# Transformer block on one core: batch 0's keys get a bank of their own, its parts are made by two engines, and the fillers read a cleared tile

## The chip, the cores and the metric

One core of one Trainium2 chip runs the whole program. The metric is the device time of one execution in microseconds (us). Most of the program is steady: one batch of sixteen takes some 12.2 us. The change touches only the head, the first 15 us or so, in which the weights arrive and batch 0 is brought to its first attention scores.

## The reference, cut to what matters

```python
mod = (silu(L0_c) @ L0_wmod).reshape(16, 6, 1, -1)
sa, ca, ga, sb, cb, gb = (mod[:, i] for i in range(6))
h = layernorm(x) * (1 + ca) + sa                  # x: 16 batches x 256 tokens x 128
qkv = (h @ Wqkv + bqkv).reshape(b, t, 3, H, HD).transpose(2, 0, 3, 1, 4)   # 16 heads of 8
q, k, v = qkv
dist2 = sum(k*k)[..., :, None] + sum(q*q)[..., None, :] - 2.0 * einsum(k, q)
x = x + ga * (einsum(exp(-dist2 * r_sigma), v) @ Wproj + bproj)
h = layernorm(x) * (1 + cb) + sb
x = x + gb * (sum over the two best of eight experts of h @ w_e.T + b_e)
```

## The kernel before, in words

Every engine has its own instruction list, written out by hand, and the engines meet at semaphores. Each list runs strictly in the order in which it is written, so a waiting instruction holds back everything behind it. `step(k)` is called on every engine for k = -2 (batch 0's first layer norm), k = -1 (batch 0's queries, keys, values and score operands) and then once per batch, k being the batch whose attention is done.

The exponent is computed by one matmul per head. For that the kernel builds `st`, which stacks for each head the rounded queries and keys ("high", fp32r), what the rounding left ("low"), and the halved negative squared norms of both, which a matmul with the constant matrix `nw` sums from `sq`. High and low parts lie in `hl` (rows 0 and 1 queries, 2 and 3 keys), the norms in `norm_hi` and `norm_parts`. For batch 0 the steps are, on the critical way:

- PE fills its waits with matmuls whose result nobody reads (`warm_up`, line 913), transposes the conditioning vector (L920), multiplies it with the modulation weights (L925), transposes the normalised batch (L1034).
- DVE turns the modulation into `shift_col` and `scale_col` (L626, L627). ACT makes `h1` from them and the transposed batch (L553).
- PE computes queries and keys into one PSUM bank, `qkv_ps` (L1000: four strips for the queries, then four for the keys), and the values into `ffn_ps` (L1009).
- DVE adds the bias columns `bqk_col` (L714, `qkf`), ACT rounds (L475), DVE squares (L639), subtracts (L641), and PE sums the squares (L1022), DVE makes `norm_hi` and `norm_parts` (L726, L731).
- Five DMAs from the queues of SP and ACT (L310, L312, L317, L484, L488) carry the parts into `st`. PE's first scores (L961) wait for all five.

The constants in between are DVE's too: `bias_columns` (L643 to L659) multiplies the identity with the bias loaded by L292 (`bq_pick`, L646), sums it to `bqk_col` (L652) and makes `nw`, `lo_col`, `be_col` and `ident_r` from the identity alone. DVE also clears the value tile `vpad` of batch 0 (L902), and POOL that of batch 1.

## Time and profile before

| | us |
|---|---|
| median of three runs (lowest, highest) | 225.71 (224.12, 226.25) |
| the profiled execution, its own time | 226.44 |
| its span, first to last instruction | 224.6 |
| outside the span | 1.84 |
| PE busy | 210.0 (93% of the span) |
| DVE, ACT, POOL busy | 174.8, 163.5, 137.3 |

The profile lists each instruction or a merged run of them with its start, its length and what released the engine. One matmul of fp32 data shows as two records. "Idle before" is what the engine waited for. The chain of waits follows the last instruction back to its releaser, step by step, and so names what set the time.

### The profile page before, as it was taken

The numbers are of one execution on the slowest core, as the hardware profiler recorded it, in microseconds if no ns is written. First come the engines' busy times: TensorE is split into PE (matmuls) and PEld (weight loads), VectorE is DVE, ScalarE is ACT, GpSimd is POOL, SyncE is SP. The second block draws the span as 40 slices with busy tenths as digits, with TensorE's granted clock in tenths as the row PEclk, the third lists the DMA queues.
The fourth block names the chain that finished last, engine by engine and source line by source line (L and its number), as shares of the span: only waits on it lengthen the run. The fifth ranks groups of instructions, "written<-read, shape, count | busy, mean of one in ns | idle before, by whom it ended". The sixth has DMA issues, their size and how long they took to land.

```text
span 224.6 us, 8205 instructions
## 1 busy us (share of the span) xinstructions
PE 210.0 (93%) x3240; PEld 150.1 (67%) x3240; DVE 174.8 (78%) x610; ACT 163.5 (73%) x234; POOL 137.3 (61%) x204
## 2 busy tenths in 40 slices
PE   7986888899999999999999999999999999999993
PEld 7653444577776767777677767676776776766792
DVE  4775441868888897988897888979888988787884
ACT  5228688877786868798777878686978777777362
POOL 5455547474866757575849577675757594435183
PEclk9997899999999999999999999999999999999999
DMA  5562424332423333434333243324242323300001
GB/s 149 149 206 99 146 87 121 117 109 84 120 85 115 95 136 86 146 90 146 92 125 93 78 128 103 118 77 149 88 148 69 140 62 107 99 23 26 3 23 48
DMA packets 22472, 22.94 MB, mean 102 GB/s; under 512 B 2330, under 2 KB 20258, under 8 KB 22434
## 3 DMA queue, kind: packets, MB, share of 16 engines
q1 hardware_dynamic: 21962, 21.79, 30.6%
q10 hardware_dynamic: 472, 0.62, 0.8%
q8 instruction: 26, 0.43, 0.8%
q14 instruction: 12, 0.10, 0.1%
HBM read 6.65 MB, written 2.12 MB: 39 GB/s over the span
## 4 chain that ended last, share of the span: by engine, by line
PE 69%; DVE 18%; issue 4%; DMA 3%; ACT 2%; SPq 1%; POOL 1%; POOLq 0%; ACTq 0%
PE att_ps L981 25%; PE qkv_ps L1000 8%; PE scores L961 7%; DVE acc L708 5%; DVE eq L787 4%; PE qkv_ps L1119 3%; PE qkv_ps L1009 3%; DMA st<-norm_parts 3%; PE scores L913 2%; DVE topi L784 2%; PE mid_ps L1083 2%; DVE x_all L746 2%; ACT probs L495 2%; PE qkv_ps L1121 2%; PE qkv_ps L1120 2%
## 5 line engine op out<-in xcount | busy, mean ns | idle before, releaser
L495 ACT ACTIVATE probs<-scores 128x1024 f32<-128x1024 f32 x128 | 124.3, 1022 | 12.8 <-PE scores L961 7.7
L981 PE MATMUL att_ps<-probs,vpad 128*32 128x256 f32 x1024 | 69.1, 386 | 0.0
L981 PEld LDWEIGHTS att_ps<-probs,vpad 128*32 128x32 f32 x1024 | 31.4, 110 | 16.9 <-issue 1.0
L961 PE MATMUL scores<-st 32*128 32x256 f32 x512 | 37.7, 331 | 4.6 <-ACT probs L495 2.7
L368 POOL TENSOR_TENSOR ve<-stats,eps 128x2 f32<-128x2 f32 x32 | 6.2, 193 | 43.4 <-DVE stats L688 43.4
L961 PEld LDWEIGHTS scores<-st 32*128 32x128 f32 x512 | 23.3, 184 | 13.8 <-ACT probs L495 4.7
L708 DVE SCALAR_TENSOR_TENSOR acc<-ffn_ps,mask,acc 128x128 f32<-128x128 f32 x114 | 32.0, 342 | 0.2
L411 POOL TENSOR_TENSOR sq<-qkf 128x512 f32<-128x512 f32 x15 | 15.6, 1040 | 24.6 <-DVE qkf L714 24.6
L375 POOL TENSOR_SCALAR xn<-x_all,stats,rstd 128x128 f32<-128x128 f32 x30 | 25.5, 853 | 1.6
L708 DVE SCALAR_TENSOR_TENSOR acc<-qkv_ps,mask,acc 128x128 f32<-128x128 f32 x64 | 18.0, 344 | 9.5 <-PE qkv_ps L1121 9.5
L370 POOL TENSOR_TENSOR rstd<-ve,expo 128x2 f32<-128x2 f32 x32 | 22.6, 707 | 2.5
L714 DVE TENSOR_TENSOR qkf<-qkv_ps,bqk_col 128x512 f32<-128x512 f32 x16 | 11.1, 692 | 12.5 <-PE qkv_ps L1000 12.5
L413 POOL TENSOR_TENSOR hl<-qkf,hl 128x512 fp32r<-128x512 f32 x15 | 19.4, 1290 | 0.8 <-DVE hl L720 0.8
L1000 PE MATMUL qkv_ps<-h,wqk_sb 128*32 128x256 f32 x256 | 18.0, 401 | 0.0
L502 ACT COPY acc<-mid_ps 128x256 f32<-128x256 f32 x15 | 5.6, 372 | 17.0 <-PE mid_ps L1083 17.0
L1119 PE MATMUL ffn_ps<-we_hi,h_hi 128*128 128x256 f32 x56 | 17.0, 304 | 0.0
L1120 PE MATMUL ffn_ps<-we_hi,h_lo 128*128 128x256 f32 x56 | 15.6, 278 | 0.0
L1121 PE MATMUL ffn_ps<-we_lo,h_hi 128*128 128x256 f32 x56 | 15.5, 278 | 0.0
L756 DVE TENSOR_SCALAR x2n<-x_all,stats,rstd 128x128 f32<-128x128 f32 x32 | 9.7, 344 | 7.5 <-POOL rstd L370 7.5
L708 DVE SCALAR_TENSOR_TENSOR acc<-att_ps,mask,acc 128x128 f32<-128x128 f32 x52 | 14.6, 342 | 0.2 <-DVE acc L708 0.2
L382 POOL TENSOR_TENSOR gated<-acc,rb_all 128x256 f32<-128x256 f32 x14 | 10.3, 734 | 5.2 <-DVE acc L708 4.5
L688 DVE BATCH_NORM_STATS2 stats<-x_all 128x6 f32<-128x256 f32 x32 | 12.4, 420 | 0.1
(170 smaller groups left out, 428.5 us busy)
## 6 DMA issues: line engine op xcount, KB each, us to landing
st<-hl SPq DMA_DIRECT2D x47, 256.0 KB
rb_all<-rb_rows SPq DMA_DIRECT2D x16, 192.0 KB, 3.2
out_dram<-x_all SPq DMA_DIRECT2D x16, 128.0 KB, 1.9
x_all<-in_L_attn_x_dram SPq DMA_DIRECT2D x13, 128.0 KB, 3.2
st<-norm_parts SPq DMA_DIRECT2D x60, 16.0 KB
we_sb<-in_L_ffn_w_experts_dram SPq DMA_DIRECT2D x1, 512.0 KB, 5.8
w_mod_sb<-in_L_wmod_dram SPq DMA_DIRECT2D x1, 256.0 KB, 5.1
st<-hl ACTq DMA_DIRECT2D x1, 256.0 KB
```

What stands on the lines that cost most here:

```text
L370: nc.gpsimd.tensor_tensor(rstd[:, n, :], ve[:, n, :], expo[:, :], ALU.pow).then_inc(rstd_ok, 1)
L375: i = nc.gpsimd.tensor_scalar(xn[:, par, t * C:(t + 1) * C], x_all[:, b, t * C:(t + 1) * C], stats[:, 0, par, 3 * t + 1:3 * t + 2], rstd[: ...
L411: nc.gpsimd.tensor_tensor(sq[:, :, :], qkf[:, :, :], qkf[:, :, :], ALU.mult).then_inc(sq_ok, 1)
L413: nc.gpsimd.tensor_tensor(hl[:, 1:4:2, :], qkf[:, :, :], hl_f[:, 0:4:2, :], ALU.subtract).then_inc(lo_ok, 1)
L495: nc.scalar.activation(probs[:, g, 2 * half:2 * half + 2, :], scores[:, 2 * half:2 * half + 2, :], ACT.Exp, scale=two_sigma).then_inc((exp ...
L708: v.scalar_tensor_tensor(acc[:, q, t, :], y, m, acc[:, q, t, :], ALU.mult, ALU.add).then_inc(acc_step, 1)
L961: i = pe.matmul(scores[:, r, t * T:(t + 1) * T], st[rows, par, g, t * P:(t + 1) * P], st[rows, par, g, T:2 * T], start=True, stop=True)
L981: i = pe.matmul(att_ps[r * ROWS:(r + 1) * ROWS, 0:T], heads[:, g * ROWS:(g + 1) * ROWS], probs[:, g, r, t * T:(t + 1) * T], start=(g == 0 ...
L1000: i = pe.matmul(qkv_ps[m, a * T:(a + 1) * T], wqk_sb[:, a, m], h1[:, :], start=True, stop=True)
L1119: pe.matmul(dst, hi, we_hi[:, es], start=True, stop=False)
L1120: pe.matmul(dst, lo, we_hi[:, es], start=False, stop=False)
L1121: i = pe.matmul(dst, hi, we_lo[:, es], start=False, stop=True)
```

## The change

1. For batch 0 the queries' bank stays `qkv_ps`, the keys go to `att_ps`, and the norm sums to bank 0 of `scores`. PE signals after the four query strips (`q0_ps`) and again after the four key strips (`qk_ps`).
2. DVE makes the queries' parts from PSUM in four instructions of 256 columns. ACT makes the keys' square and high part from PSUM, and also `norm_hi`. DVE makes the keys' low part. The bias enters each instruction as a column.
3. The seven fillers at the start (four before) and all later ones read `blank`, which DVE clears as its first act. They no longer wait for the identity. Two fillers ahead of `norms(0)` go.
4. `nw`, `lo_col`, `be_col`, `ident_r` are made right after the identity. `bq_pick` moves ahead of the modulation's columns, `bqk_col` stays behind batch 1's statistics.
5. The clearing of `vpad` for batch 0 goes from DVE to POOL. ACT doubles and loads sigma before the key parts, not after its DMAs. `turn_x(1)` waits for `lo_ok` in place of `v_ok` and `norm_ok`, and the expert transposes wait for `lo_ok` too.

```diff
+        def k_bank(b):
+            return att_ps[:, 0:T] if b == 0 else qkv_ps[:, T:2 * T]
+        def n_bank(b):
+            return scores[:, 0, :] if b == 0 else qkv_ps
         def norm_tile(b):
...
+                if b == 0:
+                    sp.wait_ge(hi0_ok, 1)
...
+                    if k == -2:
+                        nc.gpsimd.memset(vpad[:, 0, :, :, :].rearrange("p t h w -> p (t h w)"), 0.0).then_inc(vpad_ok, 1)
...
-            def high_parts():
-                act.wait_ge(qkf_ok, 1)
-                nc.scalar.copy(hl[:, 0:4:2, :], qkf[:, :, :]).then_inc(hi_ok, 1)
+            def first_keys():
+                act.wait_ge(qk_ps, 1)
+                act.wait_ge(bqk_ok, 1)
+                nc.scalar.activation(sq[:, 1, :], k_bank(0), ACT.Square, bias=bqk_col[:, 1:2]).then_inc(sq_ok, 1)
+                nc.scalar.activation(hl[:, 2, :], k_bank(0), ACT.Identity, bias=bqk_col[:, 1:2]).then_inc(hi_ok, 1)
...
             def norm_high(b):
...
-                nc.scalar.copy(norm_hi[norm_tile(b)], qkv_ps[norm_tile(b)]).then_inc(nh_ok, 1)
+                nc.scalar.copy(norm_hi[norm_tile(b)], n_bank(b)[norm_tile(b)]).then_inc(nh_ok, 1)
...
             def first_low_rows():
-                act.wait_ge(lo_ok, 1)
+                act.wait_ge(hi_ok, 1)
+                act.wait_ge(lo0_ok, 1)
...
-                    high_parts()
...
+                    act.wait_ge(sig_ok, 1)
+                    nc.scalar.reg_load(two_sigma, sig[0:1, 1:2].bitcast(U32))
+                    first_keys()
+                    norm_high(0)
...
-                    act.wait_ge(sig_ok, 1)
-                    nc.scalar.reg_load(two_sigma, sig[0:1, 1:2].bitcast(U32))
...
             def first_parts():
...
+                dve.wait_ge(q0_ps, 1)
+                dve.wait_ge(bqk_ok, 1)
+                v.tensor_scalar(qkf[:, 0, :], qkv_ps[:, 0:T], bqk_col[:, 0:1], None, ALU.add).then_inc(qkf_ok, 1)
...
-                v.tensor_tensor(sq[:, :, :], qkf[:, :, :], qkf[:, :, :], ALU.mult).then_inc(sq_ok, 1)
+                v.scalar_tensor_tensor(sq[:, 0, :], qkv_ps[:, 0:T], bqk_col[:, 0:1], qkf[:, 0, :], ALU.add, ALU.mult).then_inc(sq0_ok, 1)
+                v.tensor_scalar(hl[:, 0, :], qkv_ps[:, 0:T], bqk_col[:, 0:1], None, ALU.add).then_inc(hi0_ok, 1)
+                dve.wait_ge(hi0_ok, 1)
+                v.scalar_tensor_tensor(hl[:, 1, :], qkv_ps[:, 0:T], bqk_col[:, 0:1], hl_f[:, 0, :], ALU.add, ALU.subtract).then_inc(lo0_ok, 1)
...
-                v.tensor_tensor(hl[:, 1:4:2, :], qkf[:, :, :], hl_f[:, 0:4:2, :], ALU.subtract).then_inc(lo_ok, 1)
-            def bias_columns():
+                v.scalar_tensor_tensor(hl[:, 3, :], k_bank(0), bqk_col[:, 1:2], hl_f[:, 2, :], ALU.add, ALU.subtract).then_inc(lo_ok, 1)
+            def bias_picks():
...
-                v.tensor_reduce(nw_pick[:, :, :], ident[:, :].rearrange("p (r d g) -> p r g d", r=R, d=HD), AX.X, ALU.add).then_inc(nw_pick_ok, 1)
+            def bias_columns():
...
+            def norm_columns():
+                v.tensor_reduce(nw_pick[:, :, :], ident[:, :].rearrange("p (r d g) -> p r g d", r=R, d=HD), AX.X, ALU.add).then_inc(nw_pick_ok, 1)
+                v.tensor_reduce(lo_col[:, :], ident[:, :].rearrange("p (m i g) -> p i m g", i=2, g=G)[:, 1, :, :], AX.XY, ALU.add, negate=True).then_inc(nw_ok, 1)
+                v.tensor_reduce(be_col[:, :], ident[:, NE:2 * NE], AX.X, ALU.add, negate=True).then_inc(nw_ok, 1)
...
-                v.tensor_reduce(lo_col[:, :], ident[:, :].rearrange("p (m i g) -> p i m g", i=2, g=G)[:, 1, :, :], AX.XY, ALU.add, negate=True).then_inc(nw_ok, 1)
-                v.tensor_reduce(be_col[:, :], ident[:, NE:2 * NE], AX.X, ALU.add, negate=True).then_inc(nw_ok, 1)
...
              def queries_keys(b):
-                if b == 0:
-                    dve.wait_ge(bqk_ok, 1)
...
             def norm_rows(b):
-                dve.wait_ge(n_ps, b + 1)
-                if b == 0:
-                    v.tensor_copy(norm_hi[norm_tile(b)], qkv_ps[norm_tile(b)]).then_inc(nh_ok, 1)
...
-                v.scalar_tensor_tensor(norm_parts[tile], norm_hi[tile].bitcast(F32), lo_col[tile[0], :], qkv_ps[tile],
+                v.scalar_tensor_tensor(norm_parts[tile], norm_hi[tile].bitcast(F32), lo_col[tile[0], :], n_bank(b)[tile],
...
             def values(b):
...
-                if b == 1:
-                    dve.wait_ge(vpad1_ok, 1)
+                if b < 2:
+                    dve.wait_ge((vpad_ok, vpad1_ok)[b], 1)
...
+                    bias_picks()
...
-                if k == -1:
-                    queries_keys(k + 1)
-                if k == -1:
...
+            v.memset(blank[:, :], 0.0).then_inc(blank_ok, 1)
...
-            v.memset(vpad[:, 0, :, :, :].rearrange("p t h w -> p (t h w)"), 0.0).then_inc(vpad_ok, 1)
+            norm_columns()
...
             def warm_up(n, w=P):
...
-                    pe.matmul(scores[:, R - 1, 0:w], ident[:, :], ident[:, 0:w], start=True, stop=True)
+                    pe.matmul(scores[:, R - 1, 0:w], blank[:, :], blank[:, 0:w], start=True, stop=True)
...
             def modulation():
+                pe.wait_ge(blank_ok, 1)
+                warm_up(6)
+                warm_up(1, P // 2)
...
-                warm_up(3)
-                warm_up(1, P // 2)
...
+                pe.wait_ge(lo_ok, 1)
...
+                    dst = (qkv_ps[:, 0:T], k_bank(b))[a]
...
-                        i = pe.matmul(qkv_ps[m, a * T:(a + 1) * T], wqk_sb[:, a, m], h1[:, :], start=True, stop=True)
+                        i = pe.matmul(dst[m, :], wqk_sb[:, a, m], h1[:, :], start=True, stop=True)
+                    if b == 0 and a == 0:
+                        i.then_inc(q0_ps, 1)
...
             def values(b):
...
             def norms(b):
...
+                    pe.wait_ge(sq0_ok, 1)
...
-                    i = pe.matmul(qkv_ps[j * ROWS:(j + 1) * ROWS, tokens], nw[:, :, :, :].rearrange("p r i g -> p (r i g)"),
+                    i = pe.matmul(n_bank(b)[j * ROWS:(j + 1) * ROWS, tokens], nw[:, :, :, :].rearrange("p r i g -> p (r i g)"),
...
             def turn_x(b):
...
-                    pe.wait_ge(v_ok, b)
-                    pe.wait_ge(norm_ok, b)
+                    pe.wait_ge(lo_ok, b)
...
             def start():
...
-                warm_up(2)
```

DVE's list around batch 0's modulation and parts, before. Names are the tiles of the section above, `ld_bq` is the load of the bias, `mod_ps` the modulation's matmul.

```order
L626 COPY shift_col<-mid_ps 128x16 [waits mod_ps]
L627 TENSOR_SCALAR scale_col<-mid_ps 128x16
L688 BN_STATS stats<-x_all 128x6 [waits ld_x0]
L646 TENSOR_TENSOR bq_pick<-ident,bq_all 128x128 [waits ld_bq]
L646 TENSOR_TENSOR bq_pick<-ident,bq_all 128x128
L650 TENSOR_REDUCE nw_pick<-ident 128x16
L652 TENSOR_REDUCE bqk_col<-bq_pick 128x2 [waits bq_pick_ok]
L655 TENSOR_SCALAR nw<-nw_pick 128x4x4 [waits nw_pick_ok]
L655 TENSOR_SCALAR nw<-nw_pick 128x4x4
...
L714 TENSOR_TENSOR qkf<-qkv_ps,bqk_col 128x512 [waits bqk_ok,qk_ps]
L639 TENSOR_TENSOR sq<-qkf 128x512 [waits qkf_ok]
L641 TENSOR_TENSOR hl<-qkf,hl 128x2x256 [waits hi_ok]
```

And now:

```order
L674 TENSOR_TENSOR bq_pick<-ident,bq_all 128x128 [waits ld_bq]
L674 TENSOR_TENSOR bq_pick<-ident,bq_all 128x128
L648 COPY shift_col<-mid_ps 128x16 [waits mod_ps]
L649 TENSOR_SCALAR scale_col<-mid_ps 128x16
L720 BN_STATS stats<-x_all 128x6 [waits ld_x0]
L681 TENSOR_REDUCE bqk_col<-bq_pick 128x2 [waits bq_pick_ok]
L662 TENSOR_SCALAR qkf<-qkv_ps,bqk_col 128x256 [waits bqk_ok,q0_ps]
L664 SCALAR_TENSOR_TENSOR sq<-qkv_ps,bqk_col,qkf 128x256 [waits qkf_ok]
L665 TENSOR_SCALAR hl<-qkv_ps,bqk_col 128x256
L667 SCALAR_TENSOR_TENSOR hl<-qkv_ps,bqk_col,hl 128x256 [waits hi0_ok]
L669 SCALAR_TENSOR_TENSOR hl<-att_ps,bqk_col,hl 128x256 [waits hi_ok]
L758 SCALAR_TENSOR_TENSOR norm_parts<-norm_hi,lo_col,scores 64x256 [waits nw_ok,nh_ok]
```

The bias product went from behind batch 1's statistics to ahead of `shift_col`, and the constants from the identity left this stretch. The three 512-column instructions became five of 256 columns.

ACT's list from batch 0's `h` to the first exponent, before:

```order
L553 ACTIVATE h<-qkv_ps,shift_col,scale_col 128x256 [waits mod_sb,xt_ps]
L475 CAST hl<-qkf 128x2x256 [waits qkf_ok]
L529 ACTIVATE sig<-sig 1x1 [waits ld_sig]
L484 DMA st<-hl 32x4x512 [waits st0_ok,lo_ok]
L488 DMA st<-norm_parts 8x4x256 [waits norm_ok]
L533 TENSOR_LOAD sig [waits sig_ok]
L535 CAST be_hi<-be_sb 16x128 [waits ld_be]
L553 ACTIVATE h<-qkv_ps,shift_col,scale_col 128x256 [waits xt_ps]
```

And now:

```order
L575 ACTIVATE h<-qkv_ps,shift_col,scale_col 128x256 [waits mod_sb,xt_ps]
L549 ACTIVATE sig<-sig 1x1 [waits ld_sig]
L551 TENSOR_LOAD sig [waits sig_ok]
L494 ACTIVATE sq<-att_ps,bqk_col 128x256 [waits bqk_ok,qk_ps]
L495 ACTIVATE hl<-att_ps,bqk_col 128x256
L499 CAST norm_hi<-scores 64x256 [waits n_ps]
L505 DMA st<-hl 32x4x512 [waits st0_ok,lo0_ok,hi_ok]
L509 DMA st<-norm_parts 8x4x256 [waits norm_ok]
L557 CAST be_hi<-be_sb 16x128 [waits ld_be]
L575 ACTIVATE h<-qkv_ps,shift_col,scale_col 128x256 [waits xt_ps]
```

Sigma's two instructions went ahead of the keys, and ACT gained the square and the norms' rounding. Both score DMAs stay behind them.

PE's list at the start, before:

```order
L913 MATMUL scores<-ident 128x128 [waits ident_ok]
L913 MATMUL scores<-ident 128x128 x2
L913 MATMUL scores<-ident 128x64
L920 MATMUL ffn_ps<-ident,c_sb 128x16 [waits ld_c]
L913 MATMUL scores<-ident 128x128 x3
```

And now:

```order
L939 MATMUL scores<-blank 128x128 [waits blank_ok]
L939 MATMUL scores<-blank 128x128 x5
L939 MATMUL scores<-blank 128x64
L947 MATMUL ffn_ps<-ident,c_sb 128x16 [waits ld_c,ident_ok]
L939 MATMUL scores<-blank 128x128 x3
```

Three more fillers stand ahead of the first transposition, and the first of them waits for the cleared tile alone.

## Rows read from the trace of the kernel before

**Rows 1.** The page: busy time of the engines.

```profile
PE 210.0 (93%) x3240; PEld 150.1 (67%) x3240; DVE 174.8 (78%) x610; ACT 163.5 (73%) x234; POOL 137.3 (61%) x204
```

**Rows 2.** The chain of waits in the head: start us, us, what.

```profile
1.51 1.97 PE scores L913 x8
3.48 0.21 PE ffn_ps L920
3.69 1.58 PE scores L913 x6
...
6.44 0.85 PE scores L913 x4
7.30 1.87 PE qkv_ps L1000 x16
9.16 0.85 PE ffn_ps L1009 x16
...
11.37 0.43 DVE norm_hi L726
...
11.83 0.48 DVE norm_parts L731
...
12.33 3.02 DMA st<-norm_parts
```

**Rows 3.** The chain of waits after the head: start us, us, what.

```profile
15.90 1.04 PE qkv_ps L1000 x16
...
21.16 1.86 PE att_ps L981 x16
...
44.12 1.00 PE att_ps L981 x16
```

**Rows 4.** The timeline of the head: start, length, engine, line, out<-in, idle before.

```profile
0.72 0.20 POOL L350 MEMSET ident<- 128x128 f32 x1 [0.29 <-POOLq L1263]
...
1.94 1.12 DVE L902 MEMSET vpad<- 128x1280 f32 x1 [0.21 <-issue]
2.10 0.43 SPq L292 DMA_DIRECT2D bq_all<-in_L_attn_bqkv_dram  x1
...
5.97 0.17 DVE L626 COPY shift_col<-mid_ps 128x16 f32<-128x16 f32 x1 [0.85 <-PE mid_ps L925]
...
6.48 0.56 ACT L553 ACTIVATE h<-qkv_ps,shift_col,scale_col 128x256 f32<-128x256 f32 x1 [1.01 <-PE qkv_ps L1034]
...
6.69 0.67 DVE L646 TENSOR_TENSOR bq_pick<-ident,bq_all 128x128 f32<-128x128 f32 x2
```

**Rows 5.** The bias tile `bq_all`, its DMA.

```profile
DMA to landing us min/median/max: 4.6/4.6/4.6
```

**Rows 6.** The timeline from 8 to 13 us.

```profile
8.24 0.22 DVE L659 CAST ident_r<-ident 128x128 fp32r<-128x128 f32 x1
...
9.23 0.69 DVE L714 TENSOR_TENSOR qkf<-qkv_ps,bqk_col 128x512 f32<-128x512 f32 x1 [0.77 <-PE qkv_ps L1000]
...
9.96 0.69 DVE L639 TENSOR_TENSOR sq<-qkf 128x512 f32<-128x512 f32 x1
...
10.66 0.72 SPq L310 DMA_DIRECT2D st<-hl  x1
...
10.70 0.63 PE L1022 MATMUL qkv_ps<-sq,nw 128*32 128x256 f32 x4
...
11.43 0.61 SPq L312 DMA_DIRECT2D st<-hl  x1
...
12.33 1.28 ACTq L488 DMA_DIRECT2D st<-norm_parts  x1
...
12.72 0.40 DVE L664 TENSOR_SCALAR g_up<-scores 16x256 f32<-16x256 f32 x1
```

**Rows 7.** Windows: stretch, length, busy us and count of PE, PEld, DVE, ACT, POOL, then TensorE's granted clock, DMA share, GB/s.

```profile
17.00:20.40 3.40, 1.61 (x22) 0.89 (x22) 2.53 (x4) 2.91 (x4) 1.83 (x2) 0.97 0.17 58
20.20:23.60 3.40, 3.40 (x40) 2.06 (x44) 0.69 (x2) 2.21 (x4) 2.75 (x5) 0.50 0.63 232
```

**Rows 8.** The page's groups: ACT's copy of 256 columns out of PSUM.

```profile
L502 ACT COPY acc<-mid_ps 128x256 f32<-128x256 f32 x15 | 5.6, 372 | 17.0 <-PE mid_ps L1083 17.0
```

More of the change, by code:

```diff
@@ L57, in adaln_block @@
         ident_r = sb("ident_r", [P, P], F32R)
+        blank = sb("blank", [P, P])
         wqkv_sb = sb("wqkv_sb", [P, NQKV])
@@ L186, in adaln_block @@
         h1_ok = sem("h1_ok")
+        blank_ok = sem("blank_ok")
+        q0_ps = sem("q0_ps")
+        sq0_ok = sem("sq0_ok")
+        hi0_ok = sem("hi0_ok")
+        lo0_ok = sem("lo0_ok")
         qk_ps = sem("qk_ps")
```

## The prediction

> **What bounds the kernel now.** I read the page's busy times first: PE is busy for 210.0 of 224.6 us [rows 1], so any microsecond that PE waits or runs slowly in the head is carried to the end, since each later batch only follows the one before. Then the chain of waits in the head [rows 2]. It runs through PE nearly all the way: fillers from 1.51, the conditioning vector at 3.48, more fillers, queries and keys at 7.30, values, norm sums, then DVE's `norm_hi` and `norm_parts`, and last a DMA that takes 3.02 us from its issue at 12.33. Scores start when it has landed. After that the head's end is PE and DVE in turn, and everything behind it moves with that landing. So the question is when `norm_parts` is issued.
>
> One number in the chain is peculiar. The sixteen records of L1000 take 1.87 us for batch 0 and 1.04 us for batch 1 [rows 2, 3]. The work is the same, so in the head PE runs at the low one of its levels, 1.2 GHz, and later at 2.4. (The clock column has no sample so early, and cannot tell.) Two fillers take 0.85 us there, 0.43 each [rows 2]. The clock also fell later on: PE was busy for only 1.61 of 3.40 us between 17.0 and 20.4, and the next stretch shows a granted clock of 0.50 [rows 7], that is 1.2 GHz.
>
> **The change part by part.** All sums are against the profiled execution, 226.44 us, of which 224.6 are its span. The median of the three runs is 0.73 lower, so I carry the difference over to it.
>
> **Fillers.** They begin when DVE has cleared `blank` instead of when the identity is done. POOL clears a tile of that size in 0.20 from 0.72 on, and a tenth of L902's 1.12 would be 0.11 [rows 4]. I take 0.95 for the first filler, 0.56 earlier than 1.51. Three more of them cost 3 x 0.43 = 1.28. The transposition of the conditioning vector is behind them and comes 1.28 - 0.56 = 0.72 later, at about 4.2 in place of 3.48 [rows 2]. At the high level three would cost half, and the delay would be 0.1. So by itself this part delays the modulation by 0.1 to 0.7.
>
> **The bias product goes ahead of `shift_col`.** DVE's list now waits there for the bias. Its load is issued at 2.10 and lands 4.6 later, at 6.70 [rows 4, 5], and indeed L646 began at 6.69. The two products take 0.67, so `shift_col` starts at 7.37 and not at 5.97, whatever PE's delay up to 1.4, which it hides. Copy and scale take some 0.25, and ACT's `h` starts at 7.64 in place of 6.48. With its 0.56 the queries start at 8.24, 0.94 later than 7.30. This is the price of the change, and I hold it for certain unless the load lands at another time.
>
> **What it gives back: PE's level.** If the clock has risen by 8.24, eight matmuls take 1.04 and the four of the queries half of it, and I add 0.1 for emptying the pipe: DVE starts at 8.24 + 0.52 + 0.1 = 8.9 against 9.23 [rows 6]. If it has not, it is 8.24 + 0.93 + 0.1 = 9.3. In front of the old start stood a second bound: DVE was only done with its constants at 8.46 [rows 6]. That cover matters: an old run whose clock rose early could start the parts no earlier than 8.5.
>
> I take the early rise, because PE's filled stretch ahead of the modulation now lasts from 0.95 to about 5.6 with one small transposition in it, and in the old run the same stretch, 1.51 to 5.27, wasn't enough to raise the clock while by the sums at 10.70 four records take 0.63 and the clock is up [rows 6]. The Trainium skill, "TensorE: Matmul & The Clock Gate", section "Part 1: The HAM clock gate", states that activity releases the clock and that the window in which it is judged runs freely, so that the moment differs from run to run. By this rule the old runs differ among each other too, and the spread of 2.13 us between three runs agrees with it; the same page says that the ramp costs under 1% of a typical kernel, which would bound the part at 2.2 us.
>
> **The parts on two engines.** Before, DVE did three instructions of 0.69 and two of 0.43 and 0.48, 9.23 to 12.31 or 3.08 us [rows 2, 6]. Now it does two adds of 256 columns, nearest L664's 0.40 [rows 6], and three of the two-input kind plus `norm_parts`, each at most the 0.48 of L731 [rows 2]: 0.80 + 4 x 0.48 = 2.72, and 0.1 for the two hand-overs of its own results, 2.8. ACT's two instructions from the keys' bank are bounded by its 0.37 copy and by the 0.56 of `h` [rows 4, 8]. Taking 0.56, they end 1.12 after the keys, that is 0.42 + 1.12 = 1.6 behind DVE's start. PE's sums can start at 1.0 behind it, and take 0.63 [rows 6], ACT's `norm_hi` another 0.4 after 1.65, to 2.1. DVE reaches `norm_parts` at 2.3, so ACT and PE are hidden with 0.2 to spare. If ACT were later than that, each 0.1 would count in full. `norm_parts` ends at 8.9 + 2.8 = 11.7 against 12.31: 0.6 earlier.
>
> **The queues.** SP's first `hl` DMA waits for ACT's rounding now, at 8.9 + 1.6 = 10.5 against 10.66; the second follows behind its 0.72; the norm rows go at about 11.9 against 12.33 on SP, on ACT at 11.8. The four transfers share the DMA engines, so the gain at the landing lies between the first's 0.16 and the last's 0.6. I take 0.5, near the last, because the last landing follows ACT's 1.28 us of issue.
>
> **Costed at nothing.** The constants from the identity take the slot of L902, 1.12 us beside the wait for x. `vpad`'s clearing on POOL lies in its idle time before the second `stats`. The doubled sigma and its load end before the keys arrive, if by some 0.1: without that cover ACT's start would slip by as much as the load is late. `turn_x(1)` and the expert transposes wait for `lo_ok`, which comes before PE gets there or little after. POOL's batch 1 rows come later by 1.4 and are needed after 12.
>
> Sum: -0.5. The profiled execution would be 225.9, the median 225.71 - 0.5 = **225.2 us**. The likeliest case's own range is 224.5 to 226.0.
>
> **The rivals.**
> - **A, the fall of the clock goes away** (faster). Sixteen records of L981 took 1.86 at 21.16 and take 1.00 at 44.12 [rows 3]; in the 3.4 us at half clock PE was on the chain throughout, so up to 1.7 us are lost. A head that is packed otherwise may not fall there. For it: the stretch before the fall was half busy and sits a few tenths elsewhere now. Against it: the change leaves that stretch as it is, only earlier. It gives 225.2 - 1.7 = 223.5.
> - **B, the clock stays low** (slower). The late `h` leaves PE with a hole from about 7.2 or 7.8 to 8.24, where before fillers met the queries nearly without one; fillers of zeros may count for less. If the level is still low at 8.24, DVE starts at 9.3, the keys' parts come 0.85 behind, and with sums at the low level `norm_parts` ends at about 12.6, 0.3 later than before. If it stays low up to batch 1's queries, these cost 0.83 more and the scores ahead of them 0.5: +1.6, 227.3. It decides from the point at which L1000 for batch 0 takes more than 1.4 us.
> - **C, it gives nothing** (the same). The median before may be of runs whose clock rose early, in which the old parts began at 8.5; or the transfers, all on the same DMA engines, land when they did. Then the late `h` eats the gain: 225.7, up to 226.0.
>
> **How the numbers follow.** The forecast has 0.50, A 0.17, B 0.13, C 0.20. The range leaves out B's far half and little of A: 223.5 to 226.6. A difference of 1%, 2.26 us, is about what a measurement can tell from no change. Faster by that needs A and more than the forecast, 0.08; slower needs all of B and the fall besides, 0.05; within 1%, 0.87.
>
> **What would show it.** In the changed profile: `h` of batch 0 at 7.6 and not at 6.5, behind DVE's bias product; L1029's sixteen records in about 1.0; DVE's first part at 8.9, its parts in 2.8, `norm_parts` issued at 11.7 to 11.9; scores at about 14.9 in place of 15.35. The prediction is wrong if `h` isn't delayed, if the norm sums wait for ACT and not DVE for its own list, or if the landing stays at 15.3 though the issue moved; in either the sum of -0.5 is luck.

## The result, and the profile after

The changed kernel takes **226.19 us** (median of 16 runs, 225.08 to 227.53). The kernel before, measured beside it, takes 225.78 (16 runs, 224.05 to 229.3). The ratio is 1.0054 with a 95% interval of 1.0028 to 1.008: half a per cent slower, where 0.2% faster was forecast. The profiled execution took 226.86 us, 0.42 more than the one of before: 0.21 of it lies in the span, 224.84 against 224.63, and 0.2 outside it. Ratios here are those of the measurement's rounds, not quotients of two medians.

The chain of waits of the changed kernel, from its first instruction to the first projection of batch 0 (start us, us, what), answers to [rows 2, 3]:

```profile
1.04 3.25 PE scores L939 x14
...
4.54 0.19 ACT silu_t L477
...
4.76 0.94 DVE silu_t L637
...
6.24 1.03 PE mid_ps L952 x4
7.27 0.51 PE qkv_ps L1065 x2
7.78 0.85 PE scores L939 x4
8.63 1.01 PE qkv_ps L1029 x8
9.64 0.79 PE att_ps L1029 x8
...
10.46 0.47 ACT sq L494
10.93 0.37 ACT hl L495
...
11.38 0.72 SPq L325
...
12.14 0.61 SPq L327
...
12.80 3.10 DMA st<-norm_parts
...
21.70 1.87 PE att_ps L1009 x16
```

A new piece stands in it: 0.94 us of DVE on `silu_t`, an instruction on 128x16 elements. The landing after 12.80 ends at 15.90; before it ended at 15.35. The timeline shows the rest (start, length, engine, line, what, idle before):

```profile
4.49 1.16 POOL L418 MEMSET vpad<- 128x1280 f32 x1
...
4.76 0.93 DVE L637 TENSOR_SCALAR silu_t<-silu_t 128x16 f32<-128x16 f32 x1 [1.28 <-ACT silu_t L477]
...
6.98 0.67 DVE L674 TENSOR_TENSOR bq_pick<-ident,bq_all 128x128 f32<-128x128 f32 x2 [0.29 <-DMA bq_all<-in_L_attn_bqkv_dram]
...
7.91 0.56 ACT L575 ACTIVATE h<-qkv_ps,shift_col,scale_col 128x256 f32<-128x256 f32 x1 [1.63 <-DVE scale_col L649]
8.56 1.08 PE L1029 MATMUL qkv_ps<-h,wqk_sb 128*32 128x256 f32 x8
...
9.71 0.48 DVE L662 TENSOR_SCALAR qkf<-qkv_ps,bqk_col 128x256 f32<-128x256 f32 x1 [1.24 <-PE qkv_ps L1029]
...
12.06 0.47 DVE L758 SCALAR_TENSOR_TENSOR norm_parts<-norm_hi,lo_col,scores 64x256 fp32r<-64x256 f32 x1
...
12.80 0.87 SPq L332 DMA_DIRECT2D st<-norm_parts  x1
...
15.94 0.51 PE L989 MATMUL scores<-st 32*128 32x256 f32 x8 [1.35 <-DMA st<-norm_parts]
```

The `silu_t` instruction starts 0.27 behind POOL's clearing of `vpad` and ends 0.04 behind its end. The same operation took 0.17 us in the kernel before, at 3.94, with POOL free. The clock fell again behind the head, in stretches that answer to [rows 7] (columns as there):

```profile
17.00:20.30 3.30, 1.41 (x22) 0.60 (x16) 2.56 (x4) 2.80 (x4) 1.19 (x2) 1.00 0.06 19
20.40:23.70 3.30, 3.30 (x40) 1.84 (x36) 0.69 (x2) 2.62 (x4) 2.66 (x4) 0.50 0.69 222
```

**How the runs are read below.** Each run lists its mean granted clock. In the profiled execution it is 0.992, with one stretch of some 3.4 us at 0.50 behind the head: 1 - 0.5 x 3.4 / 224.8 = 0.992. The runs lie near such steps: 0.996 to 1.00 (no stretch after the first rise), 0.989 to 0.992 (one), 0.981 to 0.985 (two), 0.977 and less (three or more). The small differences within a step come of a low stretch at the very end, where PE has nothing left to do: e8's trace, 0.997, has no other, and it starts at 221.34 of 222.60. I count the falls of each run so, and 6.8 us in one piece count as two. All runs of the changed kernel, and all those of the old one that were measured beside an experiment:

| | runs | no fall | one | two | three or more |
|---|---|---|---|---|---|
| before | 122 | 44, median 224.37 | 68, 225.94 | 7, 226.83 | 3 |
| changed | 28 | 5, median 225.50 | 16, 226.34 | 4, 227.46 | 3, 227.30 |

In the old kernel the runs with one fall lie 1.6 us above those with none, more than the whole disputed difference, and whether a fall comes differs from run to run. Not all of the 1.6 need be the fall itself. The traces give its price apart from the head, as the time from the first scores to the end of the span: 208.0 to 208.3 us in the three without a fall (e2, e8, e9), 208.9 to 209.4 in the seven with one at 18 to 20 us, 209.8 in the three with one at 26.5 to 26.8 (e7, e10, e14), and 209.8 to 210.0 in the four with 6.8 us at half clock. So a fall at 20 us costs about 1.0, and one at 26.5 about 1.6. No run of the old kernel without a fall was traced, so what else sets those 44 runs apart stays open.

Each experiment has two readings, then: its head, from the trace, and how many of its runs had no fall.

### The profile page after: what moved, and what is told of

Read it like the earlier page. It is cut to its first block, busy times and chain, and to the rows that moved or that the text cites. A ratio compares the mean times of both kernels' runs of the same rounds, so it can differ in the third digit from the quotient of the medians.

```text
span 224.8 us, 8201 instructions
## 1 busy us (share of the span) xinstructions
PE 210.4 (94%) x3242; PEld 150.5 (67%) x3242; DVE 175.2 (78%) x611; ACT 164.0 (73%) x236; POOL 138.3 (62%) x205
## 4 chain that ended last, share of the span: by engine, by line
PE 70%; DVE 18%; issue 5%; ACT 3%; POOL 1%; DMA 1%; SPq 1%; ACTq 0%; POOLq 0%
PE att_ps L1009 26%; PE scores L989 7%; PE qkv_ps L1029 7%; DVE acc L740 5%; DVE eq L814 4%; PE qkv_ps L1150 3%; PE qkv_ps L1040 3%; DVE topi L811 2%; PE ffn_ps L1150 2%; ACT probs L516 2%; PE scores L939 2%; DVE x_all L773 2%; PE mid_ps L1114 2%; PE qkv_ps L1152 2%; PE qkv_ps L1151 2%
## 5 line engine op out<-in xcount | busy, mean ns | idle before, releaser
L744 DVE TENSOR_TENSOR qkf<-qkv_ps,bqk_col 128x512 f32<-128x512 f32 x15 | 10.4, 691 | 11.7 <-PE qkv_ps L1029 11.7
L1029 PE MATMUL qkv_ps<-h,wqk_sb 128*32 128x256 f32 x248 | 17.1, 393 | 0.0
L740 DVE SCALAR_TENSOR_TENSOR acc<-att_ps,mask,acc 128x128 f32<-128x128 f32 x52 | 14.6, 342 | 0.3 <-PE ffn_ps L1152 0.3
```

The costliest lines, as they stand in the source:

```text
L740: v.scalar_tensor_tensor(acc[:, q, t, :], y, m, acc[:, q, t, :], ALU.mult, ALU.add).then_inc(acc_step, 1)
L1029: i = pe.matmul(dst[m, :], wqk_sb[:, a, m], h1[:, :], start=True, stop=True)
```

## The experiments

Theories. **P**: POOL's clearing, new in the head, holds DVE's `silu_t` and so the modulation. **L**: `shift_col` waits behind the bias product for a load. **F**: the longer fillers delay the modulation, or pay by an early rise of the clock. **K**: the number of falls behind the head decides more than the head does. The rise of the clock, late or early, is the moment from which the trace grants PE the high level for the first time: 9.95 before, 10.13 in the changed kernel's trace. The head's marks are, in this order, the transposition of the conditioning vector, the start of the modulation, of `h`, of the norm sums, and of the scores. Before they are 3.41, 5.06, 6.48, 10.70 and 15.40; changed they are 4.22, 6.24, 7.91, 10.99 and 15.94.

### The changed kernel, one delay taken out at a time

**e1**: `vpad` is cleared later (edit of the changed kernel; `...` in brackets stands for the rest of an index).

```diff
                     rsqrt(0, k + 2, par, bn1, ve1, rstd1)
-                    if k == -2:
-                        nc.gpsimd.memset(vpad[:, 0, ...], 0.0).then_inc(vpad_ok, 1)
                     if k == -1:
                         normalise(k + 2, par)
+                        nc.gpsimd.memset(vpad[:, 0, ...], 0.0).then_inc(vpad_ok, 1)
```

> The changed kernel with one edit: POOL clears batch 0's vpad behind its own normalising of batch 1 and no longer at 4.49 us, beside DVE's silu. Theory P (POOL's clearing holds DVE's small tensor_scalar, 0.93 in place of 0.17, and that is on the critical way): the instruction is back at 0.17, the modulation's matmul starts at 5.7 in place of 6.24. P alone says scores start 0.5 to 0.75 earlier than 15.94. Theory L (the bias product, which waits for its load until 6.96, stands ahead of shift_col) says that this gains nearly nothing while L stands: shift_col stays at 7.57, h at 7.85, scores at 15.8, the time within 0.2 us of the changed kernel's.

225.86 us, ratio 1.0025 (0.9995 to 1.0056). The timeline:

```profile
4.75 0.18 DVE L635 TENSOR_SCALAR silu_t<-silu_t 128x16 f32<-128x16 f32 x1 [1.28 <-ACT silu_t L475]
...
6.37 0.66 DVE L672 TENSOR_TENSOR bq_pick<-ident,bq_all 128x128 f32<-128x128 f32 x2 [0.43 <-DMA bq_all<-in_L_attn_bqkv_dram]
...
7.29 0.56 ACT L573 ACTIVATE h<-qkv_ps,shift_col,scale_col 128x256 f32<-128x256 f32 x1 [1.02 <-PE qkv_ps L1063]
```

The 0.93 is 0.18 again: that POOL held it is shown. `h` is at 7.29, scores at 15.54, with a late rise (10.21). Part of it is luck: the bias landed at 6.35 here, at 6.96 in the changed kernel's trace. With that landing L costs nothing here, since `h` waits for PE's transposition of the batch and not for `scale_col`.

**e2**: the bias product goes back behind `shift_col`.

```diff
                     first_normalise()
-                    bias_picks()
                     modulation(0)
                 if k == -1:
+                    bias_picks()
                     bias_columns()
```

> The changed kernel with the bias product back behind batch 1's statistics. L alone says: shift_col at once when the modulation is done, 7.1 in place of 7.57, and h 1 us earlier. P and F together (F: three more fillers push the first transposition to 4.22) say that the transposed batch is then the later one: it comes at 7.78, h at 7.8, so gain of 0.1 to 0.15 only, scores at 15.8.

225.90 us, ratio 1.0041 (1.0009 to 1.0073). `silu_t` still took 0.94, yet `h` started at 7.25. In this trace the clock rose at 4.57 and the norm sums began at 9.73, though `h` was later than before. So 7.25 can't be set against the 7.91 of a late rise; the trace of e9, the changed kernel's own head with a rise at 4.75, has 7.54, and L is worth the 0.29 between them. With both edits and an early rise `h` is at 6.49 (e13), with both and a late rise at 7.29 (e14).

**e3**: three of the long fillers less.

```diff
                 pe.wait_ge(blank_ok, 1)
-                warm_up(6)
+                warm_up(3)
```

> The changed kernel with three and a half fillers at the start in place of six and a half. F alone says 1.28 us earlier from the first transposition (2.93 in place of 4.22) to the scores. With L in place: h at 7.85, as the bias lands at 6.96 whatever PE does, scores at 15.85, and the time within 0.2 us of the changed kernel's. If the longer filler stretch raises the clock earlier (the forecast's reason), this run should be slower in the head instead, with L1029's sixteen records at 1.87.

227.78 us, ratio 1.0122 (1.0075 to 1.0169): worse, though the transposition moved from 4.22 to 2.94. The timeline shows the clearing meet another instruction, `xn` (0.59 for the pair before):

```profile
3.48 0.17 DVE L637 TENSOR_SCALAR silu_t<-silu_t 128x16 f32<-128x16 f32 x1
...
4.49 1.17 POOL L418 MEMSET vpad<- 128x1280 f32 x1
4.58 1.22 DVE L654 TENSOR_SCALAR xn<-x_all,stats,rstd 128x128 f32<-128x128 f32 x2 [0.43 <-POOL rstd L385]
```

`h` gained little: it started at 7.54, behind the bias product. PE was left with a hole, 1.30 us busy of 3.30, and the next stretch ran at half clock, inside the head:

```profile
5.00:8.30 3.30, 1.30 (x13) 1.01 (x16) 2.29 (x8) 0.65 (x3) 1.02 (x3) 1.00 0.87 253
8.40:11.60 3.20, 3.20 (x37) 1.50 (x29) 2.23 (x5) 0.84 (x2) 2.01 (x3) 0.50 0.02 2
```

None of its 6 runs was without a fall. That the extra fillers of the changed kernel cover a hole which P and L make, and that three do where those are gone (e4), fits these windows. It is argued from one trace and 6 runs, not shown.

**e4**: e1, e2 and e3 together.

> The three edits together: vpad cleared later, bias product behind the statistics, three and a half fillers. If the three are the whole cause and cover each other: first transposition 2.93, modulation 4.45, h at 5.9, queries at 6.5, DVE's first part at about 8.0, scores at 14.1 to 14.5, the time about 1.2 us (0.5%) below the kernel before, 1.7 below the changed one. If the new parts on two engines are themselves at fault, scores stay at 15.4 or later.

226.01 us, ratio 1.0033 (1.0 to 1.0066). `silu_t` took 0.17, `h` started at 5.72, the norm sums at 8.52, scores at 13.47. The head is 2.5 us earlier than the changed kernel's and 1.9 earlier than the old one's, and the median did not follow. The windows say where it went:

```profile
16.90:20.30 3.40, 2.55 (x28) 1.56 (x32) 1.39 (x4) 2.87 (x5) 2.15 (x3) 0.68 0.42 140
20.30:23.70 3.40, 3.40 (x57) 1.82 (x50) 1.76 (x3) 1.25 (x2) 3.18 (x5) 0.81 0.48 169
```

The fall came 2 us earlier, and there were more: 3 of 12 runs had none (median 223.93), 2 had one (225.60), 7 had two (226.22). With no fall it beats the old kernel's 224.37 by 0.4.

**e13**: e1 and e2 together, the fillers stay.

> The changed kernel with the clearing late and the bias product behind the statistics, and the six and a half fillers at the start kept. First transposition 4.22, modulation 5.7, h at 6.6 to 7.1, scores at 14.5 with a clock that rises early, 14.9 without. Theory H (clearing and bias product together are the price of the head, the fillers are not): runs without a fall at 224.0 to 224.3, median 225.0 to 225.5, and an early first rise more often than with three fillers. If the fillers are a price of 0.8 of their own, the runs without a fall are at 224.7, 0.8 above the 223.9 of the run with all three edits.

225.94 us, ratio 1.0028 (0.999 to 1.0066). `h` was back at 6.49 and scores came at 13.93, 1.5 earlier than before, with the clock up from 4.80. No run was without a fall: 8 had one (225.25), 4 two (227.19). At one fall it is 0.7 below the old kernel's 225.94.

### The old kernel, one part of the change at a time

**e5**: only the parts, their banks, and what goes with them: the queues' new order, sigma's two instructions ahead of the keys, the new waits of `turn_x(1)` and the expert transposes, and the two fillers ahead of the norm sums gone.

```diff
+                v.tensor_scalar(qkf[:, 0, :], qkv_ps[:, 0:T], bqk_col[:, 0:1], None, ALU.add).then_inc(qkf_ok, 1)
...
-                v.tensor_tensor(sq[:, :, :], qkf[:, :, :], qkf[:, :, :], ALU.mult).then_inc(sq_ok, 1)
+                v.scalar_tensor_tensor(sq[:, 0, :], qkv_ps[:, 0:T], bqk_col[:, 0:1], qkf[:, 0, :], ALU.add, ALU.mult).then_inc(sq0_ok, 1)
...
+                nc.scalar.activation(sq[:, 1, :], k_bank(0), ACT.Square, bias=bqk_col[:, 1:2]).then_inc(sq_ok, 1)
+                nc.scalar.activation(hl[:, 2, :], k_bank(0), ACT.Identity, bias=bqk_col[:, 1:2]).then_inc(hi_ok, 1)
```

> The kernel before with only the parts and banks of the change (keys in their own bank, ACT and DVE at once, sigma's load ahead, the two fillers ahead of the norm sums gone). Constants, fillers from the identity, vpad on DVE and the bias product as before. The forecast's step on the parts: DVE starts its five instructions at 8.5 at the earliest, scores at 14.7 in place of 15.40, time 0.5 to 0.7 below the kernel before. Rival, the chain of queues (SP's first DMA waits for ACT's second instruction): scores no more than 0.3 earlier. Theory K (falls of the clock behind the head decide as much as the head): the runs without a fall are faster, but fewer, as PE waits more; the median stays within 0.3 of the kernel before.

226.64 us beside 225.81, ratio 1.0008 (0.9974 to 1.0043). Up to the queries, at 7.23, the head is the old one to 0.01 us. Then:

```profile
8.38 0.48 DVE L660 TENSOR_SCALAR qkf<-qkv_ps,bqk_col 128x256 f32<-128x256 f32 x1
...
9.23 0.47 ACT L492 ACTIVATE sq<-att_ps,bqk_col 128x256 f32<-128x256 f32 x1 [2.10 <-PE att_ps L1026]
...
10.93 0.47 DVE L756 SCALAR_TENSOR_TENSOR norm_parts<-norm_hi,lo_col,scores 64x256 fp32r<-64x256 f32 x1 [0.25 <-ACT norm_hi L497]
...
14.87 0.39 PE L986 MATMUL scores<-st 32*128 32x256 f32 x4 [1.40 <-DMA st<-norm_parts]
```

`norm_parts` starts 0.90 earlier, scores 0.53. The core of the change does what it says, though 0.37 of its gain goes on the way from `norm_parts` to the landing. But 5 of 12 runs had two falls, and only 2 none.

**e6**: only the clearing of `vpad` on POOL, where the change has it.

```diff
                     rsqrt(0, k + 2, par, bn1, ve1, rstd1)
+                    if k == -2:
+                        nc.gpsimd.memset(vpad[:, 0, ...], 0.0).then_inc(vpad_ok, 1)
...
             columns()
-            v.memset(vpad[:, 0, ...], 0.0).then_inc(vpad_ok, 1)
```

> The kernel before with one edit: vpad of batch 0 is cleared by POOL behind its first rstd, as in the changed kernel. Theory P, the clearing on POOL holds DVE's small instructions: here silu is over before it starts (4.4), but the two of xn (4.53 to 5.12) are held until about 5.5, the transposition of x comes at 6.1 in place of 5.78, scores 0.3 to 0.4 later, time +0.3. Without P: nothing changes, since DVE's 1.12 us lay beside the wait for x.

224.94 us, ratio 0.9987 (0.9945 to 1.003). The clearing is as long and at the same place, and it hits what stands there in the old order:

```profile
3.95 0.17 DVE L617 TENSOR_SCALAR silu_t<-silu_t 128x16 f32<-128x16 f32 x1 [0.58 <-ACT silu_t L462]
...
4.39 1.17 POOL L403 MEMSET vpad<- 128x1280 f32 x1
4.54 1.16 DVE L634 TENSOR_SCALAR xn<-x_all,stats,rstd 128x128 f32<-128x128 f32 x2
```

The hold of 0.57 on `xn` costs nothing: PE is on the modulation until 5.9, and every mark up to `norm_parts` is the old one. In the changed kernel P hurts because the fillers push `silu_t` from 3.94 to 4.76, into the clearing. It is the two parts of the change together. (0.3 us more had been expected of this run, from `xn`; neither the marks nor the time show it.)

**e11**: only the long fillers, from a cleared tile.

```diff
+            v.memset(blank[:, :], 0.0).then_inc(blank_ok, 1)
...
+                pe.wait_ge(blank_ok, 1)
+                warm_up(6)
+                warm_up(1, P // 2)
                 pe.wait_ge(ident_ok, 1)
-                warm_up(3)
-                warm_up(1, P // 2)
```

> The kernel before with the filler part of the change alone: blank cleared first by DVE, six and a half fillers from it at the start. Theory F: the first transposition goes from 3.41 to 4.22, h and scores 0.8 later (16.2), time +0.8 at an equal number of falls. The forecast's reason for the change, an early rise of the clock, would show as scores no later than 15.4 and a first high stretch that begins before 7 us.

225.36 us, ratio 0.9997 (0.9962 to 1.0032). The transposition was at 4.21, but `h` at 6.53 and the scores at 15.16, not at the 16.2 of theory F: the clock rose at 5.35, and the faster modulation gave the delay back. 1 of 12 runs had no fall, against 44 of 122; the 8 with one have a median of 225.25, 0.7 below the old kernel's 225.94. An early rise pays, and more falls take it back.

**e12** and **e15** are the two kernels once more, unchanged, the first for one look.

> The kernel before, a second look at it. If the clock's moment is a matter of the run (theory K), the first rise stands elsewhere than at 9.95 us, and with an early one (before 7) DVE's first part starts at 8.5, bounded by its constants, and scores at about 14.7; no fall behind would give 224.4. If it stands at 9.95 again, the moment is the program's.

> The changed kernel as it is, on the same chip as the two others. Expected from its first 16 runs: median 226.2, the runs without a fall 225.2 and some 2 in 10, those with one 226.2. If the moment of the clock is the run's, this profile may show the first rise near 4.7 and not at 10.13, and scores then at 15.0.

e12: 227.19 us, with 3.41, 5.06, 6.48, 10.64 and 15.49, and 6.8 us at half clock behind the head in place of 3.4:

```profile
19.10:22.50 3.40, 2.73 (x32) 1.47 (x36) 1.22 (x3) 2.88 (x5) 2.06 (x3) 0.51 0.41 138
22.50:25.90 3.40, 3.40 (x44) 1.83 (x40) 1.83 (x3) 0.63 (x1) 3.26 (x5) 0.50 0.42 152
```

The same code, the same head to 0.1 us, and 0.75 us more than the first profiled execution. e15: 227.19 us median, ratio 1.006 (1.002 to 1.0099), scores at 15.81. The slowdown repeats. Its first rise is at 9.82, as late as in the first trace (10.13).

### Fillers where the fall is prepared

In the traces of both kernels the fall at about 20 us comes behind 3.4 us in which PE was half idle [rows 7]. The next four kernels put small multiplications there: four or five behind the expert transposes, where PE waits for the scores' rows, and four ahead of batch 1's norm sums.

```diff
                 expert_weights()
+                warm_up(5)
...
                 if has(k - 1):
                     project(k - 1)
+                if k == 0:
+                    pe.wait_ge(wr_sb_ok, 1)
+                    for _ in range(4):
+                        pe.matmul(att_ps[:, 0:P], blank[:, :], blank[:, 0:P], start=True, stop=True)
                 if has(k + 1):
                     norms(k + 1)
```

**e7**, on the old kernel (`warm_up(4)`, and `ident` in place of `blank`):

> The kernel before with four more fillers while PE waits for batch 0's score operands (some 14.3 to 15.3) and four more ahead of batch 1's norm sums (18.4 to 19.6, into att_ps once wr_t is copied). Theory K: the clock falls at about 20 since PE had little to do before; with eight fillers there, 0.22 us each at the high level, the falls become rare and the median comes down from 225.2 to 225.7 towards that of the runs without a fall, 224.4: 0.5 to 0.9 lower. Without K: nothing, or up to 0.3 slower where a filler is in the way.

**e9**, on the changed kernel (`warm_up(4)`):

> The changed kernel with the eight late fillers alone (four before the first scores, four ahead of batch 1's norm sums); its head is untouched. Theory K with H (H: the head itself is late by the bias product, the clearing and the first fillers): scores stay at 15.9, falls go in most runs, and the median is that of the changed kernel's runs without a fall, 225.2, which is 0.8 above the same runs of the kernel before (224.4). If K is wrong the median stays at 226.2. If H is wrong, the no-fall runs come to 224.4.

**e8**, on e4:

> The run with all three edits, and late fillers as well: five while PE waits for the score operands, four ahead of batch 1's norm sums. With three edits alone the runs without a fall took 223.9 and were 3 of 12, the others 226.2 in the middle. Theory K: most runs are without a fall now, the median is 224.0 to 224.5, 0.5% below the kernel before. If K is wrong the median stays at 226.

**e14**, on e13:

> The same with nine late fillers. Theory K: falls at 17 to 20 go, falls at 26 may stay; median 224.3 to 224.8, below the kernel before by 0.5% and as good as or better than the best so far (224.73 beside 225.81).

| | with late fillers | ratio to before (95%) | runs without a fall: without the late fillers, with them |
|---|---|---|---|
| e7, old | 225.06 | 0.9982 (0.9942 to 1.0023) | 44 of 122; 7 of 12 |
| e9, changed | 225.64 | 1.0027 (0.9986 to 1.0068) | 5 of 28; 7 of 12 |
| e8, on e4 | **224.73** | **0.9951 (0.9913 to 0.9989)** | 3 of 12; 8 of 12 |
| e14, on e13 | 224.79 | 0.9982 (0.9942 to 1.0023) | 0 of 12; 7 of 12 |

(One run of e9 of 641.21 us was disturbed and stands in neither its ratio nor in what I conclude, though the count of 7 holds it.) The windows of e8 beside those of e4 above:

```profile
16.90:20.30 3.40, 3.24 (x42) 2.29 (x46) 2.26 (x5) 2.65 (x4) 2.19 (x3) 1.00 0.33 102
20.30:23.70 3.40, 2.81 (x60) 1.44 (x51) 2.25 (x3) 2.51 (x4) 3.22 (x4) 1.00 0.56 197
```

In each of the four pairs the share of runs without a fall is higher with them. For the three on the changed kernel it is 22 of 36 against 8 of 52, by multiplications that compute nothing. So what PE does between 13 and 20 us decides on these falls, as K says. e8 beats the kernel before by 0.5%, and by the ratios to it the changed one as well. It is the only one of the four whose interval lies below 1, and of thirteen variants measured in rounds the best, so a part of the 0.5% may be chance. Falls at about 26.5 remain: they are in the traces of e7, e10 and e14, behind the stretch that was filled.

**e10**: e8 with three more fillers ahead of batch 0's norm sums and one behind `turn_x(0)`.

> The best run so far (three edits and nine late fillers, 224.73) with three fillers more ahead of batch 0's norm sums, where PE waits some 0.6 at the high level, and one more ahead of the queries. Theory K: still fewer falls, median 224.1 to 224.5. Rival: PE has no hole there at the low level, so each filler pushes the norm sums by 0.2 to 0.4, and the median is 0.2 to 0.5 higher.

226.20 us beside 225.91, ratio 1.0001 (0.9962 to 1.004), 5 of 12 without a fall (224.31, as e8's 224.40), scores at 15.42 against e8's 14.33. More of the same, on the path itself, gave the gain back.

## Why the prediction was wrong

The time was inside the range, 223.5 to 226.6, and within 1% of the old one, to which 0.87 was given. The forecast itself, 0.5 us faster, was wrong in sign: the ratio's interval lies above 1. Its own range, up to 226.0, missed by 0.2. By its steps:

- **The fillers.** First filler at 1.04 (0.95 forecast), transposition at 4.22 (4.2). Right. But this delay was taken to vanish behind the wait for the bias, and it didn't: see the next two.
- **The bias product.** There is such a wait: DVE's 0.29 of idle time ahead of it is ended by the load, `shift_col` follows, and `h` is at 7.91 (7.64). The load landed at 6.96, not 6.70; I held its landing for fixed by one trace, and in the 17 of the study it lies between 5.47 and 7.04. But the step says that the late `shift_col` hides whatever PE brings up to 1.4, and there it failed. 1.4 is the slack of `shift_col`; `h` itself waited for PE's transposition of the batch already before [rows 4], and its slack is 1.16. In e15, the same kernel with the bias landed at 6.30, `h` is still at 7.82, and it waits for PE's transposition of the batch:

```profile
7.32 0.17 DVE L648 COPY shift_col<-mid_ps 128x16 f32<-128x16 f32 x1
...
7.82 0.57 ACT L575 ACTIVATE h<-qkv_ps,shift_col,scale_col 128x256 f32<-128x256 f32 x1 [1.54 <-PE qkv_ps L1065]
```

  PE's own path came 1.34 later, by the fillers and by what was costed at nothing, and so was as late as the bias. `h` by what stands in the head and by the rise of the clock:

| in the head | `h`, late rise | `h`, early rise |
|---|---|---|
| the old start | 6.48 (before, e12) | none traced |
| six and a half fillers | 7.29 (e14) | 6.49 (e13), 6.53 (e11) |
| those and the clearing on POOL | | 7.25 (e2) |
| those and the bias product ahead | 7.29 (e1) | |
| all three | 7.91, 7.82 (changed, e15) | 7.54 (e9) |

  The rows of e14 and e13, in this order:

```profile
7.29 0.56 ACT L573 ACTIVATE h<-qkv_ps,shift_col,scale_col 128x256 f32<-128x256 f32 x1 [1.01 <-PE qkv_ps L1063]
...
6.49 0.57 ACT L573 ACTIVATE h<-qkv_ps,shift_col,scale_col 128x256 f32<-128x256 f32 x1 [0.19 <-PE qkv_ps L1063]
```

  With a late rise, by the table, 0.8 of the 1.4 us is the fillers, 0.5 the clearing, and the bias only the last 0.1.
- **"Costed at nothing: `vpad`'s clearing on POOL lies in its idle time."** Wrong as reasoning. POOL was idle, but the clearing stops an instruction of DVE on the critical chain: 0.94 in place of 0.18. The Trainium skill, "SBUF — State Buffer", section "Who interferes with whom", says that a `tensor_scalar` in a two-port mode of DVE and GpSimd take a shared pair of ports from each other, and that whichever came second is fully blocked until the other's instruction ends. The traces agree: at three places (0.93 here, 1.16 in e6, 1.22 in e3) DVE's instructions start behind the clearing and end 0.04 to 0.14 after it does. In which mode they ran no row shows.
- **"I take the early rise"**: this step failed in the profiled execution. The clock was first up at 10.13. The queries started at 8.56 and DVE 1.15 later, where 0.66 was forecast. The text had priced a low clock at 0.4. The late start of 0.32 and this 0.49 put DVE's first part at 9.71 in place of 8.9. It is not wrong for every run: in e2, e3, e4, e9, e11 and e13 the rise came at 4.5 to 5.4, in the changed kernel's two traces and in e1, e8, e10 and e14 at 9.4 to 10.2. e9, whose head is the changed kernel's own, had it at 4.75 and its scores near the 14.9 of the forecast:

```profile
7.54 0.56 ACT L575 ACTIVATE h<-qkv_ps,shift_col,scale_col 128x256 f32<-128x256 f32 x1 [1.26 <-DVE scale_col L649]
...
14.97 0.51 PE L989 MATMUL scores<-st 32*128 32x256 f32 x8 [0.31 <-DMA st<-norm_parts]
```

  With the same code up to the norm sums, e13 (early) and e14 (late) have the scores at 13.93 and 15.46: 1.5 us of the head hang on it, and the forecast should have carried both. Whether the change makes the early rise more frequent is open. It is in none of the five traces with the old start (before, e5, e6, e7, e12) and in six of the twelve with fillers from `blank`, which could be chance. Even where it comes it doesn't decide the comparison: e9's six undisturbed runs without a fall have a median of 225.18, the old kernel's 44 have 224.37, and its 7 with late fillers (e7) 224.79. The text also took the 2.13 us between three old runs for a sign that the rise moves; by the counts above falls alone can make such a spread.
- **The parts.** 9.71 to 12.53 is 2.82 (2.8). ACT's second ended 1.59 behind DVE's start (1.6, though 0.42 + 1.12 is 1.54). The norm sums waited 0.17 for ACT's square, which the text names as a sign of being wrong, but DVE went from its list into `norm_parts` with 0.04 between, so the cover held. In e5 it did not quite: DVE waited 0.25 for ACT's `norm_hi`. The core edit alone gave -0.53 at the scores, as forecast.
- **The queues.** The last landing took 3.10 (3.02). SP's norm rows went at 12.80, 0.27 behind the end of `norm_parts`, because both `hl` DMAs stood ahead of them on SP and the first had waited for ACT to 11.30. I had them at 0.2 behind. From the start of `norm_parts` to the scores it is 3.88 us, and 3.57 before. I had put 0.1 there, and it is 0.3.
- **Outside the span.** The text carried the 1.84 us outside the span over unchanged. The time less the span is 1.82 on average in the old kernel (1.81 to 1.83 in e6, e7 and e11), and 1.98 to 2.04 in the changed one and every kernel with its parts on two engines, e5 too. So 0.2 us come with that part of the change, before the first instruction or behind the last. What makes them was not looked for.

Together, for the two profiled executions: `h` came 1.43 later, the way from `h` to `norm_parts` took 1.20 less, and from there to the scores 0.31 more, which is the 0.54 by which the scores are late. In e15 against e12 it is 1.34, 1.16 and 0.14, or 0.32. The steps that failed are the delay of `h`, forecast at 1.16, with the clearing at nothing in it, and the early rise, a gain of 0.4 in the sum that did not come.

- **The falls.** Rival A asked whether the fall goes away, and nothing asked whether falls become more frequent. The old kernel's runs had 0.75 falls each, the changed one's 1.2. At 1.0 to 1.6 us each that is 0.4 to 0.7 us, of a difference between the overall medians of 1.15 (226.79 against 225.64). The rest is the head (scores 0.54 and 0.32 later) and the 0.2 outside the span; in runs with none, one or two falls the medians are 0.4 to 1.1 apart. That the change itself makes falls more frequent isn't shown: 5 of 28 without one against 44 of 122 could be chance. Late fillers' effect on them could hardly be.

The rivals: B came nearest. The clock stayed low past the queries, as it says, and rose before batch 1's; its `norm_parts` at 12.6 was 12.53. But its reason was other than the hole, since PE's level in the first 9 us differs between executions of one code, and other than the zeros in the fillers, which all six early rises had too. Its decision point named L1000's sixteen records; they took 1.80 here, and 1.87 before, so by its own sign B had arrived. C was right that the late `h` eats the gain, not on the size; that the old median is of runs with an early rise no trace shows.

**What stays open.** Whether the early rise pays in the end: its traces have earlier scores (15.80 in e3, whose clock fell again in the head, is the exception), but in e3, e4, e11 and e13 the later falls are many, and e11 comes out level. Of e4's 1.9 us in the head only 0.4 are left even in the runs without a fall. Of this, 0.2 lie outside the span. For another part the 1.9 sets an early rise against a late one: the old runs without a fall have a span of 222.6, and less 208.0 to 208.3 their scores would be at 14.3 to 14.6 and not at 15.40, an estimate that no trace of such a run confirms. And the separate prices of P and L in time: e1 and e2 gained 0.1 to 0.3% on the changed kernel, inside their intervals.

## What to carry to other kernels

Before an instruction is moved to an idle engine, look at what the neighbour that shares its memory ports does in those microseconds, and which of its instructions stands on the chain; the same clearing cost nothing in the old order, and in the new one it held a link of the chain for 0.76 us and made `h` 0.5 later. A delay that is to hide behind a wait must be summed with all others on its path before it is called hidden. Where a kernel starts cold, read the granted clock of every run: an edit that ends the head 2 us earlier moved the median by nothing until the half-idle stretch behind it was filled. And compare runs with an equal number of falls before crediting or blaming an edit of a few tenths of a microsecond.

## What the runs showed of the hardware

- The moment at which the clock first rises fell, in executions of nearly the same head, either at 4.5 to 5.4 us (six traces) or at 8.9 to 10.2 (eleven), none between.
- One fall of the clock, 3.4 us at half of it, costs about 1.0 us of 225 where it comes at 18 to 20 us and 1.6 at 26.5 (first scores to the end: 208.2 on average without, 209.2 and 209.8 with it), and runs of one program differ by it (224.37 and 225.94, 44 and 68 runs): more than most edits to this kernel are worth.
- Small multiplications in the two half-idle stretches ahead of it raised the runs without a fall from 8 of 52 to 22 of 36.
- A DVE instruction of 0.17 us was held to 0.93 by a POOL clearing of 1.16 us; another, L689 of 0.24 for the pair, took 0.89 beside a POOL copy of 1.04 us.
- A load of 192 KB, issued at the same place, landed between 5.47 and 7.04 us.
